# Attention loop on TensorE: half of the output projection moved between the two halves of the scores, the Q projection behind both

## What is computed

```python
xn = layernorm(x)
out = x + attn(xn) + ffn(xn)

# attn: 16 heads of 64; each block of 64 query rows sees 64 selected keys
qkv = xn @ Wqkv + bqkv
scores = einsum('bhnmd,bhnsd->bhnms', q[mrm] * scale, k[idx0])
sexp = exp(scores - max(scores)); acc = sexp @ v[idx0]
attn = (acc / (1e-6 + sum(sexp))) @ Wproj + bproj

# ffn: FP4 quantize and dequantize (blocks of 16) of inputs and weights
h = silu(q4(xn) @ q4(w_gate).T) * (q4(xn) @ q4(w_up).T)
ffn = q4(h) @ q4(w_down).T
```

## Time and profile before

| what | value |
|---|---|
| time, median of 3 runs | 1647.01 us (1644.1 to 1647.72) |
| the profiled execution's own time | 1641.71 us |
| its span on the slowest core (core 3) | 1640.1 us (the other cores 1627.6 to 1634.6) |
| mean granted TensorE clock of the 8 cores | 0.959 to 0.964 of full speed |
| PE busy | 1378.2 us (84%) |
| DVE busy | 1138.1 us (69%) |
| ACT busy | 941.5 us (57%) |
| POOL busy | 190.6 us (12%) |

### The profile page before, as it was taken

One profiled execution on the slowest core, in us unless ns is written; L12 is line 12 of the kernel. 1 busy time (PEld: TensorE's weight loads), 2 busy tenths in 40 slices (PEclk: granted clock), 3 DMA queues, 4 the chain that ended last, 5 costly groups with the idle time before them and its releaser, 6 DMA issues.

```text
span 1640.1 us, 26596 instructions; the slowest of 8 cores (1627.6 to 1640.1 us)
## 1 busy us (share of the span) xinstructions
PE 1378.2 (84%) x8976; PEld 722.2 (44%) x8976; DVE 1138.1 (69%) x1561; ACT 941.5 (57%) x1603; POOL 190.6 (12%) x202
## 2 busy tenths in 40 slices
PE   0004748899899988769999999999999999999997
PEld 0002333565566655324444444444444444444443
DVE  3587643687776877638868677686868778686855
ACT  1356645788878888636555545555554545555542
POOL 1100130333333332000000000000000000000000
PEclk9999769999999999789999999999999999999999
DMA  9988684677887876794453555546463555545343
GB/s 193 267 271 262 200 199 131 158 189 180 196 181 182 202 178 182 178 198 81 97 117 92 117 107 108 119 97 130 86 122 94 119 108 101 126 98 118 79 101 91
DMA packets 257351, 240.29 MB, mean 147 GB/s; under 512 B 203906, under 2 KB 206978, under 8 KB 257218
## 3 DMA queue, kind: packets, MB, share of 16 engines
q1 hardware_dynamic: 217634, 120.69, 32.7%
q0 software_dynamic: 17056, 52.84, 16.7%
q10 hardware_dynamic: 22528, 65.05, 12.4%
HBM read 145.97 MB, written 52.20 MB: 121 GB/s over the span
## 4 chain that ended last, share of the span: by engine, by line
PE 55%; DVE 0%; DMA 0%; issue 0%; DVEq 0%; ACT 0%; SPq 0%; ACTq 0%
PE psG L926 19%; PE psV L933 19%; PE psD L948 18%; DMA hqT<-wc 0%; DVE sg L1023 0%; DVE wc L1044 0%; DVE am L1028 0%; DVE rs L1038 0%; DVE pp L1000 0%; DVEq L864 0%; ACT su L984 0%; DVE sg L1041 0%; DVE hsc L1035 0%; DVE wc L1031 0%; DVEq L998 0%
## 5 line engine op out<-in xcount | busy, mean ns | idle before, releaser
L926 PE MATMUL psG<-wgqT,xqT 128*128 128x512 bf16 (+1 forms) x1536 | 336.9, 362 | 14.9 <-PEq L230 14.9
L933 PE MATMUL psV<-wuqT,xqT 128*128 128x512 bf16 (+1 forms) x1536 | 335.6, 361 | 0.0
L948 PE MATMUL psD<-wdqT,hqT 128*128 128x512 bf16 x1408 | 316.8, 381 | 4.0 <-DMA hqT<-wc 4.0
L926 PEld LDWEIGHTS psG<-wgqT,xqT 128*128 128x128 bf16 x1536 | 150.6, 98 | 176.3 <-issue 16.8
L933 PEld LDWEIGHTS psV<-wuqT,xqT 128*128 128x128 bf16 x1536 | 150.3, 98 | 154.0 <-issue 0.2
L984 ACT COPY su<-psV 128x512 f32<-128x512 f32 (+1 forms) x192 | 105.7, 551 | 193.2 <-PE psV L933 193.2
L980 ACT ACTIVATE sg<-psG 128x512 f32<-128x512 f32 (+1 forms) x192 | 107.9, 562 | 186.3 <-PE psG L926 186.2
L948 PEld LDWEIGHTS psD<-wdqT,hqT 128*128 128x128 bf16 x1408 | 138.3, 98 | 166.1 <-issue 8.3
L1000 DVE TENSOR_TENSOR pp<-psD,pp 128x512 f32<-128x512 f32 x64 | 41.2, 686 | 208.3 <-PE psD L948 208.3
L364 PE MATMUL psR<-ident,wdqT 128*128 128x128 bf16 x320 | 29.4, 246 | 164.9 <-DMA wdqT<-xn_dram,kidx 156.8
L408 PE MATMUL psR<-wdqT 128*128 128x256 bf16 x1024 | 137.6, 297 | 7.3 <-issue 5.8
(11 more groups left out here) (92 smaller groups left out, 1730.5 us busy)
## 6 DMA issues: line engine op xcount, KB each, us to landing
wgqT<-xin SPq DMA_DIRECT2D x32, 512.0 KB, 10.9
partial_dram<-po ACTq DMA_DIRECT2D x32, 512.0 KB, 5.6
pp<-partial_dram SPq DMA_DIRECT2D x32, 512.0 KB, 4.4
pp<-xin POOLq DMA_DIRECT2D x32, 512.0 KB, 6.3
out<-pp SPq DMA_DIRECT2D x32, 512.0 KB, 2.6
xb<-xin SPq DMA_DIRECT2D x30, 512.0 KB, 4.1
wrow<-wg ACTq DMA_DIRECT2D x22, 512.0 KB
wrow<-wu ACTq DMA_DIRECT2D x22, 512.0 KB
```

The lines of the kernel that those rows point to most:

```text
L926: m = tensor.matmul(psG[g % 3][:, 0:iw], xqT[t % 2][:, k, :], wgqT[:, k, HU * half + i0:HU * half + i0 + iw], start=(k == 0), stop=(k == N ...
L933: m = tensor.matmul(psV[g % 3][:, 0:iw], xqT[t % 2][:, k, :], wuqT[:, k, HU * half + i0:HU * half + i0 + iw], start=(k == 0), stop=(k == N ...
L948: m = tensor.matmul(psD[oc][:], hqT[u % 3][:, k, :], wdqT[:, HB * half + k, 512 * oc:512 * (oc + 1)], start=(half == 0 and k == 0), stop=( ...
```

## The change

P1 leaves its place right behind P0 and goes behind S0; S1 follows P1; Q comes behind S1. All instructions, operands, semaphores and waits stay as they are, and so does the order of the users of the three banks (T, P0, P1, Q, Q, A). No other engine's program changes.

```diff
                         if 0 <= J - 2 < NJ:
                             proj(J - 2, 0)
+                        if J + 1 < NJ:
+                            scores(J + 1, 0)
+                        if 0 <= J - 2 < NJ:
                             proj(J - 2, 1)
                         if J + 1 < NJ:
-                            scores(J + 1, 0)
+                            scores(J + 1, 1)
                         if q_step(J)[0] < NJ // 2:
                             q_half(*q_step(J))
-                        if J + 1 < NJ:
-                            scores(J + 1, 1)
```

## The result

| what | before | changed |
|---|---|---|
| median of 4 runs each | 1647.37 us | 1724.24 us |
| ratio | | 1.0452, 95% interval 1.0418 to 1.0486 |
| the profiled execution: own time, span | 1641.71, 1640.1 us | 1725.13, 1723.5 us |
| granted clock of the 8 cores | 0.959 to 0.964 | 0.943 to 0.951 |
| first scores matmul to last, mean of 8 cores | 388.2 us | 460.8 us |

By the ratio the change makes the kernel 4.5% slower, 74 us, to 1721.8 us; 1726.5 us was forecast.

The account below looks back on a forecast made before the run. A ring through T, its copy, E, S0 and PE's work until the next T, as tight as PE's own work, bounds the loop. 41.5 + 31 (clock) + 7 (loop's end) = +79.5 us, giving 1726.5 us, range 1705 to 1740.

Parts of the forecast that it names:

- the ring through T, its copy, E and S0: Attention loop: T, its copy on ACT, E, S0, then PE's work until the next T; 11.79 us, as tight as PE's work.
- The sum: Whole kernel: 41.5 us for order at full clock, 31 for low clock, 7 for the loop's end, together +79.5 us.
- the 24 intervals: Loop from S0 of step 2 to S0 of step 26: 306.1 us before, 347.6 forecast at full clock, 9 steps with two passes.
- P1's 2.14 us in every step: PE in the loop: P1 behind S0 makes the next T 2.14 us later; the wait before S0 grows from 0.35 to 2.49.
- A step of 13.93 us, one of 15.4: S0 to S0 at full clock in the changed loop: 13.93 us with one weight pass, 15.4 us with two.
- Q's new place costs nothing: Loop, Q behind S1: Q and S1 only trade places inside the ring, cost nothing; nb stays about 0.7 us ahead of E.
- The clock, 31 us: Idles before S0 bring PE's clock down: 1.45 us in nine of ten of 24 steps, 31 us; bounds 0 and 34.8.
- The end of the loop, +2.7 to +7.1: Three intervals from S0 of step 26 to S0 of step 29: 36.7 us before, 39.4 forecast, or 43.8 with low clock.
- the clock did not hold: Rival that the clock holds, leaving P1's move alone in the loop: +44 us, 1691 us; chance 0.15.
- it was low for longer: Rival that the low clock lasts longer, each loop step losing some 3 us, or nb comes last: +120, 1767 us; chance 0.11.
- faster by the sooner S1: Rival that the sooner S1 lets E start sooner in the 9 long steps: 26 us less, 1621 us; chance 0.02.
- its lower end: Whole kernel: the forecast's own range of 1705 to 1740 us starts at 1705, with half of the steps at the low clock.

Follow-up runs that it names:

- the second profile: The changed kernel run again unaltered for a second profile: 1718.4 to 1726.9 us, ratio 1.0467 to the kernel before.
- the filled experiment: Changed kernel with useless copies of P1's first matmuls (8, or 17 behind a step with two weight passes) between P0 and S0: 1690.4 and 1691.6 us.
- the first experiment: Kernel before with only Q moved, behind S1, and P1 still ahead of S0: 1687.9 to 1694.2 us in the second series, ratio 1.0309.
- the sixth experiment: Kernel before with Q moved behind S1, P0 and P1 ahead of S0, and E ahead of the copy of T on ACT: 1676.9 us in one run.
- the fifth experiment: Changed kernel with E put ahead of the copy of T on ACT: 1698.6 to 1704.2 us in four runs, ratio 1.0362 to the kernel before.

## Why the prediction was right

- **What bounds the kernel**: the ring through T, its copy, E and S0. Right. P1 behind S0 lengthens it (+67 us of loop alone), a second half lengthens it again, other work in the same place does the same, and taking the copy of T out of it makes the kernel faster than before.
- **The sum**: 79.5 us forecast, 72.6 more in the loop (73.1 in the second profile). In the mean of the cores the 24 intervals went from 302.2 to 364.9 us, +62.7 for 72.5 forecast, and the three behind them from 35.3 to 40.4, +5.0 for the 7 in the sum. The steps ahead of step 2 grew by 1.5 us and what follows S0 of step 29 by 3.4, and both were put at nothing: at the last pair of scores P1 now stands between S0 and S1, 4.64 us apart on core 1 (741.17 and 745.81), where they were 0.60 apart. So 12 us too much and 5 too little partly cancel, and that the time came within 5 us is in part luck.
- **P1's 2.14 us in every step**: right. The idle before S0 went from 0.35 to 2.49 us.
- **A step of 13.93 us, one of 15.4**: 13.54 and 15.34 measured at full clock. The short one was 0.4 too long. I read the rows on the slowest core, core 3, where Q took 3.95 us because its weight loads stood still for 0.38 us in the middle. Core 0 of the same kernel has Q at 3.67, as the changed kernel has; first core 3's weight loads, then Q on core 0:

```profile
441.08 0.99 PEld L408 LDWEIGHTS psR<-wdqT 128*128 128x128 bf16 x10 [0.38 <-issue]
```

```profile
432.99 3.67 PE L408 MATMUL psR<-wdqT 128*128 128x256 bf16 x32
```

  What held core 3's loads is not shown; it is not the copies of P0 and P1, which end at 438.84. So the 24 intervals at full clock come to 15 x 13.54 + 9 x 15.34 = 341.2 us, +35 against core 3 before, where +41.5 was forecast; the filled experiment's 342.4 on core 5 is 39 more than core 5 had before (303.2). Both differences take the low clock of the kernel before along, as the forecast's did.
- **Q's new place costs nothing**: nearly. 0.1 us gained in a step and some 6 us of loop lost at a lower clock, in the changed kernel; 2 to 7 us of loop by itself on the second die, and much more on the first, by a wait of S1 that the forecast did not know. `nb` was 0.5 us ahead of E in a long step, for 0.7 forecast.
- **The clock, 31 us**: 24 us over the 24 intervals (365.2 less 341.2), 25 in the loop by the filled experiment. The size is near, the count was wrong. I said that nine in ten steps would pay 1.45 us. 11 of 24 did. All nine behind an idle of 3.8 us or more paid 1.6 to 2.0; of the fifteen idles of 2.49 us only two did, but these two steps cost 4.4 us (17.91) and 3.9 (19.25). It is so on all cores of both profiles: 9 of 9 long idles, and 1 to 4 of 15 short ones. The price of 1.45 was low, since 4.24 from S0 to S1 was core 3's figure and the others show 3.97 at full clock.
- **The end of the loop, +2.7 to +7.1**: +3.8 (40.5 us from S0 of step 26 to that of step 29).
- **The rivals**: the clock did not hold, and it was low for longer in two steps of 24, not in all. Nothing got faster by the sooner S1: the first and the sixth experiment show 5 us at most, with E's place changed.
- **The range**: its lower end, half of the steps at the low clock, comes to 1709 us by the forecast's own terms, not 1705.

The forecast set aside the advice of the Trainium skill (TensorE: Matmul & The Clock Gate, "Why this matters for your kernels") that only a longer gap brings the clock down. For the short steps it came closer than I did: 13 of 15 idles of 2.49 us left the clock up. Yet low stretches stand in the trace of before behind idles of 1.85 and 1.87 us, and behind three of 1.40 and 1.41.

## What to carry to other kernels

If an engine waits for almost nothing before one instruction, ask what stands ahead of it: it may be just as long as a ring through other engines, and then its place is worth its whole length in every round. Follow the ring through the fixed order of each engine, not only through the data: E did not need T, it only stood behind T's copy on ACT, and that swap was the gain to be had here (0.7%, and 1.2% with the idle filled). Price a longer wait on TensorE twice, once as time and once as clock: here 25 us of the changed kernel's loop were low clock, of which some 10 were not there before. And read a step on more than one core: the slowest had a stall in it that the others had not.

## What was not expected of the hardware

- Work that is thrown away made the kernel faster, twice: 25 us of loop in the changed kernel (460.8 to 436.3), 6 us in the one with E first (377.4 to 371.0).
- The length of the idle before S0 does not decide alone whether the clock falls: 7 of 10 idles from 1.4 to 2.4 us had a low stretch behind them in the kernel before, and 2 of 15 of 2.49 us in the changed one. What else does was not tried.
- A wait of TensorE for its own semaphore, directly behind the matmuls that raise it, took 0.15 to 0.3 us in most steps on the cores of one die and up to 2.4 on those of the other, on two chips (the first experiment). It is not tied to that die: in step 1 of the changed kernel, where no P1 stands between S0 and S1, it took 1.6 to 2.05 us on the cores of the second die and at most 0.2 on those of the first. Ahead of the loop it took 0.15 on every core. Core 6 of the changed kernel:

```profile
303.59 0.64 PE L427 MATMUL psS<-QT,Ks 64*64 64x64 bf16 x16 [2.05 <-remote]
```

  With 2 us of work between, no such wait of over 0.9 us is left from step 2 on, except in the fifth experiment, where the first die was longer too. No run takes the wait away, and its cause stays open.
